# The node's own term in graph attention: added at the end on VectorE, or weighed early on ScalarE into the bank that collects the sum

## The reference, cut to what matters

```python
h = (x @ W).reshape(n, HEADS, OUT_DIM)
e = leaky_relu(a_src[src] + a_dst[dst], 0.2)
m = segment_max(e, dst)
e = exp(e - m[dst])
denom = segment_sum(e, dst)
alpha = e / (denom[dst] + 1e-16)
out = segment_sum(h[src] * alpha[:, :, None], dst)
out = out.reshape(n, 256) + bias
x = layernorm(x + gamma * norm(out) + beta)
```

## Time and profile before

| | |
|---|---|
| runs | 2984.63, 2986.3, 2990.3 us (median 2986.3) |
| profiled execution | 2984.63 us, its span 2982.8 us |
| TensorE busy | 2465.0 us, 83% |
| VectorE busy | 1409.8 us, 47% |
| ScalarE busy | 674.1 us, 23% |
| GpSimd busy | 947.8 us, 32% |
| mean granted TensorE clock | 0.917 of full speed |

### The profile page before, as it was taken

How to read it: one execution, slowest core, us unless ns; L and a number is a source line. 1 busy time by engine, 2 the same in 40 slices (tenths; PEclk the granted TensorE clock), 3 DMA queues, 4 the chain that set the end, 5 groups by cost and what they waited for, 6 DMA issues and landing times. The chain is left out here.

```text
span 2982.8 us, 32239 instructions
## 1 busy us (share of the span) xinstructions
PE 2465.0 (83%) x9483; PEld 1620.8 (54%) x9484; DVE 1409.8 (47%) x3952; ACT 674.1 (23%) x1372; POOL 947.8 (32%) x939
## 2 busy tenths in 40 slices
PE   3677788898897999999999999999975777677750
PEld 2444788344675555565556555577732334465540
DVE  7999665455674001030101001455573555676658
ACT  3777544111443000010001000254400000100002
POOL 0000256676666000000000000011267666477650
PEclk9888989898998999999999999999987898798885
DMA  6565677343344744434443434333558788466631
GB/s 232 245 251 228 212 247 247 114 142 115 94 121 133 155 152 131 156 126 155 134 151 126 155 119 140 103 100 102 107 190 269 244 280 257 153 213 187 187 108 43
DMA packets 209629, 493.88 MB, mean 166 GB/s; under 512 B 46553, under 2 KB 128526, under 8 KB 209230
## 3 DMA queue, kind: packets, MB, share of 16 engines
q1 hardware_dynamic: 135281, 301.30, 32.2%
q10 hardware_dynamic: 38173, 133.27, 12.8%
q0 software_dynamic: 36032, 57.60, 7.1%
HBM read 374.71 MB, written 117.32 MB: 165 GB/s over the span
## 5 line engine op out<-in xcount | busy, mean ns | idle before, releaser
L791 POOL DMA_INDIRECT table_dense_weights<-pair_weight,dst x416 | 415.4, 999 | 561.6 <-DVE weights_c L846 324.6
L1523 PE MATMUL banks<-own_term,features_and_rows 128*128 128x391 f32 (+1 forms) x1656 | 552.3, 491 | 0.0
L2128 POOL DMA_INDIRECT features_and_rows<-table_heads,src x376 | 405.7, 1079 | 207.3 <-issue 112.0
L1523 PEld LDWEIGHTS banks<-own_term,features_and_rows 128*128 128x128 f32 x1656 | 312.2, 189 | 226.8
L1549 DVE TENSOR_SCALAR features_and_rows<-banks,hop_bias 128x391 f32<-128x391 f32 (+1 forms) x24 | 15.0, 625 | 760.4 <-PE banks L1523 760.4
L951 PE MATMUL banks<-split_rows,count_columns 128*128 128x512 f32 x1200 | 323.3, 416 | 19.9 <-ACT count_columns L933 16.6
L2540 PE MATMUL banks<-features_and_rows,edge_to_window 128*128 x880 | 226.9, 419 | 71.0 <-DVE edge_to_window L2501 28.2
L1523 PE MATMUL banks<-features_and_rows 128*128 128x391 f32 (+1 forms) x840 | 282.4, 491 | 0.0
L951 PEld LDWEIGHTS banks<-split_rows,count_columns 128*128 128x128 f32 x1200 | 229.2, 195 | 75.0 <-ACT count_columns L933 14.9
L557 PE MATMUL banks<-features_and_rows,pair_and_bias_rows 128*128 128x400 f16 x806 | 182.5, 386 | 88.6 <-DVE features_and_rows L539 50.5
L933 ACT CAST count_columns<-hidden 128x640 fp32r<-128x640 f16 x310 | 213.4, 723 | 153.7 <-PE banks L951 42.5
(11 more groups left out here) (422 smaller groups left out, 2997.2 us busy)
## 6 DMA issues: line engine op xcount, KB each, us to landing
hidden<-table_counts SPq DMA_DIRECT2D x305, 160.0 KB
table_dense_weights<-weights_c ACTq DMA_DIRECT2D x26, 1600.0 KB, 5.7
own_term<-table_dense_weights SPq DMA_DIRECT2D x52, 782.0 KB
features_and_rows<-table_rows_by_edge SPq DMA_DIRECT2D x58, 528.0 KB
own_term<-table_dense_weights SPq DMA_DIRECT2D x34, 780.5 KB
pair_and_bias_rows<-table_edge_rows ACTq DMA_DIRECT2D x50, 512.0 KB
weights_c<-table_edge_rows ACTq DMA_DIRECT2D x50, 512.0 KB
table_rows_by_edge<-features_and_rows SPq DMA_DIRECT2D x48, 528.0 KB
```

The lines of the kernel that those rows point to most:

```text
L791: e.indirect_dma_start(out=self.table, out_offset=bass.IndirectOffsetOnAxis(ap=self.place[:, t:t + 1], axis=0), in_=self.values[:, t:t + 1 ...
L1523: m = e.matmul(psum[b][:, 0:wide], z_block(block)[:, f * P:(f + 1) * P], streamed[tile % STREAM][:, lo - from_column:lo - from_column + wi ...
L2128: e.indirect_dma_start(out=to[:, k, :], out_offset=None, in_=t_h, in_offset=bass.IndirectOffsetOnAxis(ap=src[:, t:t + 1], axis=0)).then_in ...
```

## The change

The own term moves from the end of the merge to its beginning, and from VectorE to ScalarE.

- On GpSimd `gather_last` and `weigh_own` stand ahead of the direct quads from 16 on, in place of behind the last quad. The 25 picks follow each other with no waits on s_mm; the exponent is made in one go of 128x200.
- On SyncE one DMA brings all own rows into `own` as soon as the weights are made, behind the reloads of the first 16 places and ahead of those from quad 16 on. The seven loads at the end are gone.
- ScalarE makes the exponential once, when node tile 4 is summed. From node tile 8 on (OWN_LATER) it begins a bank with own row times weight, in eight activations of 33 columns (one a head), in place of zeros. For node tiles 0 to 7 the sums go to `first_sums` (free parts of `hidden` and `w_a`), and ScalarE scales the own rows in place, eight activations a tile, so in each of the turns 4 to 11 sixteen activations stand where one copy stood.
- In the closing pass VectorE's multiplication of the own rows is gone for all groups, and the addition is left for groups 0 and 1 alone.

```diff
@@ gather_rows
             gather_direct(e, [q for q in DIRECT_QUADS if 2 * IN_CHAIN <= q < PLACES])
+            gather_last(e)
+            weigh_own(e)
             gather_direct(e, [q for q in DIRECT_QUADS if q >= PLACES])
-            gather_last(e)
@@ gather_last, weigh_own
-            for g, tiles_of in enumerate(OWN_GROUPS):
-                for j in tiles_of:
-                    if j % 2 == 0 and j <= FIRST_OWN * GROUP:
-                        e.wait_ge(s_mm, mm0 + MERGE_STEPS - 4 * (FIRST_OWN * GROUP - j))
-                    e.indirect_dma_start(out=mx[:, j, :], out_offset=None, in_=t_run,
-                                         in_offset=bass.IndirectOffsetOnAxis(ap=last_at[:, j:j + 1], axis=0)).then_inc(s_last[in_part(g)], 16)
-                if g == FIRST_OWN:
-                    for some in range(FIRST_OWN):
-                        weigh_own(e, some)
-            for g in range(FIRST_OWN, len(OWN_GROUPS)):
-                weigh_own(e, g)
+            for j in range(NODE_TILES):
+                e.indirect_dma_start(out=mx[:, j, :], out_offset=None, in_=t_run,
+                                     in_offset=bass.IndirectOffsetOnAxis(ap=last_at[:, j:j + 1], axis=0)).then_inc(s_last, 16)
+
+        def weigh_own(e):
+            e.wait_ge(*g_last)
+            e.tensor_tensor(mx, own_score, mx, ALU.subtract).then_inc(s_own_max, 1)
+            e.wait_ge(s_own_max, 1)
+            e.tensor_tensor(own_gap, mx, mask[:, :].unsqueeze(2).broadcast_to([P, NODE_TILES, HEADS]), ALU.mult).then_inc(s_own_gap, 1)
@@ attention_sp
+            e.wait_ge(*weights_made)
+            e.dma_start(own[:, :, :], t_h.rearrange("(t p) d -> p t d", p=P)).then_inc(s_own_back, 16)
             for quad in [q for q in STAGED_QUADS if q >= PLACES]:
                 load_rows(e, quad)
-            for g in range(len(OWN_GROUPS)):
-                load_own(e, g)
@@ merge_act
+            def weigh(to, d, signal):
+                for h in range(HEADS):
+                    of = slice(h * HEAD_ROW, (h + 1) * HEAD_ROW)
+                    done = e.activation(to[:, of], own[:, d, of], ACT.Copy, scale=p_self[:, d, h:h + 1])
+                done.then_inc(signal, 1)
+
             for d in range(NODE_TILES):
                 e.wait_ge(s_mm, e.snap(ends_of_node[d], min_val=1, max_val=MERGE_STEPS + UNROLL))
-                e.copy(own[:, d, :], node_bank(d)).then_inc(s_summed, 1)
+                e.copy(first_sums[d // GROUP][:, d % GROUP, :] if d < OWN_LATER else own[:, d, :], node_bank(d)).then_inc(s_summed, 1)
                 if d + SUM_BANKS < NODE_TILES:
                     e.wait_ge(s_summed, d + 1)
-                    e.copy(node_bank(d + SUM_BANKS), no_sums).then_inc(s_begun, 1)
+                    if d + SUM_BANKS < OWN_LATER:
+                        e.copy(node_bank(d + SUM_BANKS), no_sums).then_inc(s_begun, 1)
+                    else:
+                        if d + SUM_BANKS == OWN_LATER:
+                            e.wait_ge(s_own_gap, 1)
+                            e.wait_ge(s_own_back, 16)
+                            e.activation(p_self, own_gap, ACT.Exp).then_inc(s_self, 1)
+                            e.wait_ge(s_self, 1)
+                        weigh(node_bank(d + SUM_BANKS), d + SUM_BANKS, s_begun)
+                        if d + SUM_BANKS < 2 * OWN_LATER:
+                            weigh(own[:, d + SUM_BANKS - OWN_LATER, :], d + SUM_BANKS - OWN_LATER, s_own_scaled)
@@ attended
-            by_head = own_rows(n).rearrange("p t (h c) -> p (t h) c", c=HEAD_ROW)
-            t = V(lambda e: e.tensor_tensor(by_head, by_head, tiles(p_self, g).rearrange("p t h -> p (t h)").unsqueeze(2)
-                                            .broadcast_to([P, len(g) * HEADS, HEAD_ROW]), ALU.mult),
-                  p_made[0], (s_own_back[in_part(n)], 16 * (len(OWN_GROUPS) - FIRST_OWN if in_part(n) else FIRST_OWN)))
-            t = V(lambda e: e.tensor_tensor(tiles(own, g), tiles(own, g), own_rows(n), ALU.add), (s_summed, g[-1] + 1), t)
-            t = V(lambda e: e.tensor_scalar(den, tiles(h_rows, g)[:, :, :, HEAD_DIM], 1e-16, None, ALU.add), t)
+            t = None
+            if g[-1] < OWN_LATER:
+                t = V(lambda e: e.tensor_tensor(tiles(own, g), tiles(own, g), first_sums[g[0] // GROUP][:, :, :], ALU.add),
+                      (s_own_scaled, g[-1] + 1), (s_summed, g[-1] + 1))
+            t = V(lambda e: e.tensor_scalar(den, tiles(h_rows, g)[:, :, :, HEAD_DIM], 1e-16, None, ALU.add), (s_summed, g[-1] + 1), t)
```

More of the change, by code:

```diff
@@ L54 @@
 SUM_BANKS = 4
+OWN_LATER = 8
 STEPS_A_LOAD = 20
@@ L2052, in residual_gnn @@
         pr.count[s_tab.name] = w_h[1]
+        s_own_back = pr.sem("own_rows_back")
         begun_rows = (s_begun_rows, 2 * 16 * NODE_TILES)
@@ L2098, in residual_gnn @@
         held_seen = pair_rows[:, 4 * DIM:4 * DIM + 2 * COLS].rearrange("p (b n) -> p b n", b=2)
+        first_sums = [at.rearrange("p (t c) -> p t c", c=ATT_ROW) for at in (
+            hidden[:, SCAN_LEN:SCAN_LEN + GROUP * ATT_ROW], w_a[:, 0:GROUP * ATT_ROW])]
         table = pair_weight[:, :].bitcast(BF16)[:, 0:TERMS * 2 * PICKED_ROWS].rearrange("p (q c n) -> p q c n", q=TERMS, c=2)
@@ L2434, in residual_gnn @@
         own_gap = tmp[:, 1, 0:NODE_TILES * HEADS].rearrange("p (t h) -> p t h", h=HEADS)
-        OWN_GROUPS = [range(lo, min(lo + GROUP, NODE_TILES)) for lo in range(0, NODE_TILES, GROUP)]
-        FIRST_OWN = 2
-        s_last = [pr.sem(f"segment_max_landed{b}") for b in range(2)]
-        s_own_back = [pr.sem(f"own_rows_back{b}") for b in range(2)]
-        in_part = lambda g: int(g >= FIRST_OWN)
+        s_last = pr.sem("segment_max_landed")
         s_own_max = pr.sem("own_maximum_made")
         s_own_gap = pr.sem("own_exponent_made")
-        own_rows = lambda g: place[PLACES // 2 + g][:, 0:len(OWN_GROUPS[g]), :]
+        s_self = pr.sem("own_weight_made")
+        s_own_scaled = pr.sem("own_rows_scaled")
         def gather_last(e):
@@ L2447, in gather_last @@
             e.wait_ge(*rows_known)
[L2448 to L2471 removed]
+            for j in range(NODE_TILES):
[6 more added lines that the diff above has]
+            e.tensor_tensor(own_gap, mx, mask[:, :].unsqueeze(2).broadcast_to([P, NODE_TILES, HEADS]), ALU.mult).then_inc(s_own_gap, 1)
+        g_last = (s_last, 16 * NODE_TILES)
         def attention_sp(e):
@@ L2560, in residual_gnn @@
         pr.queue["dve"].append(merge_dve)
-        weighed, p_made = {}, [None]
+        weighed = {}
         def attended(g):
             den = tiles(a_dst, g)
-            n = g[0] // GROUP
-            if n in (0, FIRST_OWN):
-                part = slice(g[0], FIRST_OWN * GROUP if n == 0 else NODE_TILES)
-                p_made[0] = A(lambda e: e.activation(p_self[:, part, :], own_gap[:, part, :], ACT.Exp),
-                              (s_own_gap, FIRST_OWN if n == 0 else len(OWN_GROUPS)))
-            by_head = own_rows(n).rearrange("p t (h c) -> p (t h) c", c=HEAD_ROW)
-            t = V(lambda e: e.tensor_tensor(by_head, by_head, tiles(p_self, g).rearrange("p t h -> p (t h)").unsqueeze(2)
-                                            .broadcast_to([P, len(g) * HEADS, HEAD_ROW]), ALU.mult),
-                  p_made[0], (s_own_back[in_part(n)], 16 * (len(OWN_GROUPS) - FIRST_OWN if in_part(n) else FIRST_OWN)))
-            t = V(lambda e: e.tensor_tensor(tiles(own, g), tiles(own, g), own_rows(n), ALU.add), (s_summed, g[-1] + 1), t)
-            t = V(lambda e: e.tensor_scalar(den, tiles(h_rows, g)[:, :, :, HEAD_DIM], 1e-16, None, ALU.add), t)
+            t = None
[3 more added lines that the diff above has]
+            t = V(lambda e: e.tensor_scalar(den, tiles(h_rows, g)[:, :, :, HEAD_DIM], 1e-16, None, ALU.add), (s_summed, g[-1] + 1), t)
             t = V(lambda e: e.reciprocal(den, den), t)
```

11 lines of the change are left out of this document (removed).

## The result

The changed kernel takes 3010.43 us (median of 4 runs, 3007.92 to 3016.49), the kernel before in the same session 2987.74 (4 runs, 2984.63 to 2990.3): ratio 1.008, 95% interval 1.0061 to 1.0098. It is slower by 22.7 us, 0.8%, where the forecast said 7.5 us. Its profiled execution took 3005.63 us (span 3003.8, granted clock 0.913), 21.0 us above the profiled one of before.

What follows compares the result with a forecast made beforehand. It took GpSimd's gathers to bound the merge until quad 38, then VectorE and TensorE with stalls, and VectorE the closing pass. Merge +33.0 less 25.5 gave +7.5 us, 2993.8 us; range 2971 to 3011.

Steps and rivals of the forecast that it cites:

- The closing pass, -25.5: Closing pass on VectorE: idle time ahead, own-row operations and a later wait go, 25.5 us less in all.
- steps a, b, c: Closing pass on VectorE: initial idle time -9.3 us, multiplications and additions -14.2, wait behind the second exponential -2.0.
- GpSimd, 34.8 us in front: GpSimd ahead of quad 16: 25 picks, a landing and two operations delay the 156 gathers by 34.8 us, bounds 34.1 to 36.7.
- VectorE finishes quad 15 and stands still until about 2660.7: Merge, VectorE: one standstill of some 35 us behind quad 15, waiting for quad 16's rows.
- the prediction's own sign: Merge, quad 16: the prediction is wrong if the standstill there is much shorter than 35 us.
- So quad 38 shifts with GpSimd's queue: +33.0: Merge, quad 38: it comes 33.0 us later, the 34.8 us less 1.8 no longer waited for a free place.
- I take them as unchanged: merge +33.0: Merge, quads 38 to 102: 49.5 us of VectorE stalls stay, so the merge is 33.0 us longer, bounds +2.9 and +58.
- Rival 1: Merge: fewer stalls, GpSimd the bound all through, under 36 us of stall; faster, at the floor -22.6 us; chance 0.20.
- rival 2: Merge: stalls of 36 to 42 or 44 us, no measurable change, 2980 to 2988 us; chance 0.13.
- Load and activations at nothing: Merge: the 3.4 MB load (18 us) hides under the standstill, the 200 activations in ScalarE's idle time; 0 us.
- Rival 4: Merge: ScalarE becomes the bound or holds the banks, needing over 0.74 us an activation; chance 0.03.
- "The change touches only the last stage": Everything ahead of the last stage: taken as unaffected, only the last stage was split and priced.

Runs made afterwards that it cites:

- the pair with the masks: Kernel before and changed kernel, both with five loaded wait values masked (`& (COLS - 1)` or `& 31`), same result: mean 3002.3 and 3011.2 us.
- v_unpaced: Kernel before, masked, without the waits on s_mm that spread the picks at its end: 3020.91 us, ratio 1.0097.
- a_spread: Changed kernel, masked, with three or four picks ahead of each of seven direct quads, 16 to 30: 2800.96 us, ratio 1.0016, signals on time.
- e_idle: Kernel before, masked, with 50 plain GpSimd subtractions ahead of quad 16 and no early picks: 2831.74 us, ratio 1.0123, signals on time.
- b_again: Kernel before with only the five wait values masked: 3001.36 us, ratio 1.0012; repeats 2 and 3 took 3000.23 and 3004.66 us.
- a_again: Changed kernel with only the five wait values masked: 3018.35 us, ratio 1.0086; repeats 2 and 3 took 3008.11 and 3007.63 us.
- a_spread2: The kernel of a_spread run again in a session with late signals: 3017.38 us, ratio 1.0074 to the kernel before.
- v_grouped: Changed kernel, masked, with the picks in seven groups over the whole merge, exponential group by group: 2804.46 us, ratio 1.0025, signals on time.
- e_load: Kernel before, masked, plus the early load of own rows, ScalarE waiting for it, late loads kept: 3001.14 us, ratio 1.0038.
- a_nopicks: Changed kernel, masked, without the 25 picks, exponent from own_score less itself: 2974.14 us, ratio 0.9932; its repeat took 2984.28 us, 0.9973.
- a_again3: Third session's run of a_again, late signals: 3007.63 us, ratio 1.008 to the kernel before.

## Why the prediction was wrong, point by point

The forecast was +7.5 us. The timed pair gave +22.7; the pair with the masks, over 56 executions, gave +8.9. The terms of the sum held in the main. The step that failed is the last of this list: that nothing differs ahead of the last stage, and that a measurement tells 6 us. By the steps of the sum:

- **The closing pass, -25.5** (steps a, b, c). Right: -25.6 in the profiled pair, and 100.0 to 100.2 against 74.2 to 74.6 us in all the traces but v_unpaced's, with late signals or without.
- **GpSimd, 34.8 us in front.** Right to 1.3 us: 33.5 by the timeline. A pick took 0.944 us, below the 0.987 I used; in a_spread, beside a working VectorE, it took 1.036. The lines of GpSimd in after and in a_spread (count, busy us, mean ns):

```profile
L2451 POOL DMA_INDIRECT tmp<-table_running_max,row_of_last_edge x25 | 23.6, 944 | 7.6 <-issue 7.6
L2456 POOL TENSOR_TENSOR tmp<-dst,tmp 128x200 f32<-128x200 f32 x1 | 0.6, 603 | 1.4 <-DMA tmp<-table_running_max,row_of_last_edge 1.4
L2458 POOL TENSOR_TENSOR tmp<-tmp,has_edges 128x200 f32<-128x200 f32 x1 | 0.5, 532 | 0.1
```

```profile
L2456 POOL DMA_INDIRECT tmp<-table_running_max,row_of_last_edge x25 | 25.9, 1036 | 7.6 <-issue 7.6
```

  The difference, 2.3 us for 25 picks, goes with one kind of VectorE's work. The scaling takes its weights from `hidden`, in on-chip memory, for quads at even places, and from `banks`, in PSUM, for the others. In after, two gathers beside the one and the other:

```profile
2676.83 1.24 DVE L2484 TENSOR_TENSOR features_and_rows<-features_and_rows,banks 128x1056 f32<-128x1056 f32 x1
2676.89 0.94 POOL L2132 DMA_INDIRECT features_and_rows<-table_heads,src  x1 [0.30 <-issue]
...
2682.17 1.25 DVE L2484 TENSOR_TENSOR features_and_rows<-features_and_rows,hidden 128x1056 f32<-128x1056 f32 x1
2682.23 2.01 POOL L2132 DMA_INDIRECT features_and_rows<-table_heads,src  x1 [0.30 <-issue]
```

  Over the merges of all 20 traces, gathers and picks together, none of the 2489 that met no scaling from `hidden` took more than 1.05 us, and 683 of the 1299 that met one did, up to 2.04 us. In a_spread 14 picks met one and took 1.11 us on average; the other 11 took 0.94. The Trainium skill, "SBUF — State Buffer", section "SBUF: two separate sides", has a VectorE operation with both inputs in SBUF, the on-chip memory, hold ports that it shares with GpSimd against a GpSimd operation that reads there. The traces agree, if the issue of an indirect DMA is such a read; the prediction put the rule on VectorE's work as a whole, which is too wide. Leaving it out for the picks was right: in after none of the 25 met such a scaling. The two operations on 200 columns took 0.603 and 0.532 us, where the sum has 0.6 us for each; that "0.6" and the bound "0.25" stand there without their unit, us.
- **"VectorE finishes quad 15 and stands still until about 2660.7".** Right with signals on time (e_idle). With late ones it came otherwise, and by the prediction's own sign this step was wrong: quad 16's scaling had no wait. In the traces with the picks in one block the standstill lies at three or four quads between 5 and 13, and in after quad 16's gather starts 4.20 us later for it.
- **"So quad 38 shifts with GpSimd's queue: +33.0".** Missed in the profiled pair, near for the kernels with masks. The trace of before has quad 38's scaling 90.6 us behind "start" (2683.22 - 2592.63), the changed kernel 131.9: 41.3 us later. But the seven other late traces without early picks have it at 100.2 to 107.4 us, 104.1 on average, and the eight with the picks in one block at 131.5 to 135.6, 133.6 on average: 29.5 us later.
- **"I take them as unchanged: merge +33.0".** Here the profiled pair was lucky. Between quads 38 and 102 the changed kernel took 171.6 us where before took 184.3, 12.7 less, and this covers the miss at quad 38; so its merge is 29.2 us longer, near the forecast, by two errors that cancel.

```profile
2741.94 1.25 DVE L2484 TENSOR_TENSOR features_and_rows<-features_and_rows,hidden 128x1056 f32<-128x1056 f32 x1
...
2913.53 1.25 DVE L2484 TENSOR_TENSOR features_and_rows<-features_and_rows,hidden 128x1056 f32<-128x1056 f32 x1
```

  Over the other traces the step stands: b_again, 2 and 3 took 174.2 to 190.5 us for this stretch, a_again, 2 and 3 175.4 to 184.5. Over all traces with late signals but v_unpaced's and a_spread2's the merge is 300.5 us on average without early picks (seven: 290.0 to 312.1) and 328.1 with them in one block (eight: 319.2 to 335.0): +27.6. Rival 1 needed under 19.5 us (25.5 - 6), rival 2 up to 31.5. Without early picks the kernel gains 21.6 us, and with them it is slower in every session with late signals, which rules rival 1 out there and leaves rival 2's upper end possible. With signals on time GpSimd is the bound all through, the condition of rival 1. Its gain did not come in a_spread and v_grouped; the changed kernel itself was not run so, and the kernel before has no trace in that condition.
- **Load and activations at nothing.** Right as far as the runs go: e_load's merge lies within those of b_again, and a_nopicks, which has both, has merges of 291.5 and 306.3 us beside b_again's 291.7 to 312.1. Rival 4 fell with 0.275 to 0.308 us an activation.
- **"The change touches only the last stage", so what lies ahead stands in the sum with nothing, and "a measurement of this kernel tells about 0.2%, 6 us, from no change".** This is the step that failed. In the profiled pair 17.4 of the 21.0 us lie ahead of "start" and only 3.6 in the last stage (390.2 against 393.8 us). The place "start", ahead of everything the change touches, lies anywhere between 2592.6 and 2611.7 in the late traces, and the profiled execution of before, on which the sum stands, has the earliest of all. And the masks, which change a little register work and nothing else, make the kernel before 11.4 us longer (3002.3 - 2990.9, interval 7.7 to 15.1, or 0.38%), while the changed kernel with masks (3011.2) is where it is without (3010.43). The four executions of each kernel agree within 6 to 9 us, but executions of the kernel before spread over 2967 to 3009 us in the other sessions with late signals.

So of the 15 us above the forecast some 11 are what the kernel before has over its own copy with masks, which are two kernels without the change. They are hardly scatter: by the means they are there in each of the three sessions (6.1, 10.8 and 17.7 us), and against all 79 late executions of the kernel before, the changed kernel is 20 us longer, with masks or without (the latter from four executions only). Why the kernel before does so well stays open. Its one trace is at "start" 15 to 18 us ahead of the three of b_again, and has quad 16's scaling 33.2 us behind "start" where they have it at 42.4 to 43.4. Two of the five masks are in the merge itself, and no run took them out one by one.

## What to carry to other kernels

Work put ahead of gathers in the queue that feeds the pipeline cost about its full time in that queue here, though GpSimd was busy for a third of the kernel only: 33.5 us in front (30.5 and 34.3 us by the timed kernels) bought 25.6 us at the end. Freeing the last engine of a pass was worth what its own timeline said, so price both sides from the timeline and not from busy shares. And before trusting a small difference, cut both traces at marks ahead of the change, and time a copy of the kernel with an edit that does next to nothing: here such an edit moved the kernel by 0.4%.

## What the runs showed of the hardware that I had not expected

- The "remote" waits came and went with the session, not with the program. In one session there were none in any of three traces, and the kernel before took 2797.7 us in place of about 2991, 6.5% less; 157 us of it lie ahead of the last stage ("start" 2435.5 against 2592.6 at the earliest). The closing pass, in which TensorE does next to nothing, takes 100.0 us either way. The granted clock was 0.935 to 0.937 against 0.902 to 0.917; whether that is cause or effect no run tells.
- In that condition the executions of the kernel before spread by 16 us (23 of them), otherwise by 16 to 42 us in a session (12 to 32 executions).
- A late signal is longer beside early picks: with early picks the longest "remote" wait on VectorE's one-hots in the merge was 14.3 to 20.5 us in eight of nine traces (10.1 in a_again3), without them 8.0 to 9.4 in seven. It seems to cost little where VectorE would stand still anyway for quad 16; v_unpaced, where it would not, is some 19 us slower than b_again (3020.91 - 3002.3). What holds the signals back was not found.
- GpSimd issues an indirect DMA in 0.94 to 0.99 us unless VectorE multiplies two inputs from on-chip memory at that time; then about half of them take longer, up to 2.04 us. A multiplication with one input in PSUM, or the one-hots with one, lengthened none.
